# The order of attention on TensorE, planned by a step-by-step model of three engines

## What is computed

```python
qh, kh, vh = heads(layernorm(x) @ Wq.T + bq), heads(ctx @ Wk.T + bk), heads(ctx @ Wv.T + bv)
scores = einsum('bhqd,bhkd->bhqk', qh, kh) * 32 ** -0.5
scores = where(arange(3202)[None, :] <= arange(4096)[:, None], scores, -inf)   # causal
x = x + (einsum('bhqk,bhkd->bhqd', softmax(scores), vh)) @ Wo.T + bo
x = x + ffn(layernorm(x))    # encoder, top-2 of 8 experts, decoder, layernorm
```

## Time and profile before

| | us |
|---|---|
| median of the runs (3) | 3200.46 |
| lowest and highest | 3199.2 and 3202.05 |
| profiled execution, its own time | 3196.54 |
| its span, first to last instruction | 3194.9 |
| TensorE, VectorE, ScalarE, GpSimd busy | 2996.2, 1813.1, 1518.6, 1620.7 |

### The profile page before, as it was taken

The page is one execution under the profiler, slowest core; times in us unless marked ns, Lnnn a source line. Parts: engine busy times, 40 slices in busy tenths (PEclk is TensorE's granted clock), DMA queues, the critical chain, the costliest instruction groups (busy, mean ns, idle before and its releaser), DMA issues. The chain is left out here.

```text
span 3194.9 us, 42271 instructions
## 1 busy us (share of the span) xinstructions
PE 2996.2 (94%) x15688; PEld 1722.8 (54%) x15688; DVE 1813.1 (57%) x3439; ACT 1518.6 (48%) x2861; POOL 1620.7 (51%) x699
## 2 busy tenths in 40 slices
PE   7977999999999999999999999996858999999996
PEld 6865555554455554555544555532644666555653
DVE  3365888875687774788755788701642333233333
ACT  2232355666555666556666556663224333433332
POOL 1011167779567799467787577797531110111110
PEclk9988799999999999999999999997978999999998
DMA  4559234458544559344568344454983110111000
GB/s 184 201 182 269 77 101 115 113 121 177 142 116 105 122 120 208 108 116 101 122 146 170 110 118 98 112 117 122 321 270 89 53 53 1 53 54 53 27 27 14
DMA packets 133283, 384.04 MB, mean 120 GB/s; under 512 B 12224, under 2 KB 28096, under 8 KB 111584
## 3 DMA queue, kind: packets, MB, share of 16 engines
q0 software_dynamic: 36192, 222.05, 26.9%
q1 hardware_dynamic: 90048, 148.07, 17.0%
q10 hardware_dynamic: 6848, 11.31, 1.2%
HBM read 124.03 MB, written 79.17 MB: 64 GB/s over the span
## 5 line engine op out<-in xcount | busy, mean ns | idle before, releaser
L859 ACT ACTIVATE pT<-s_bank 128x512 f32<-128x512 f32 (+5 forms) x2176 | 1088.7, 581 | 722.7 <-PE s_bank L1019 548.0
L878 DVE TENSOR_REDUCE row_max<-m_bank 128x1 f32<-128x512 f32 (+4 forms) x2240 | 1258.5, 626 | 296.0 <-PE m_bank L972 166.0
L797 POOL TENSOR_TENSOR part_sum<-part_sum,pT 128x2048 f32<-128x2048 f32 x236 | 1103.3, 4675 | 119.4 <-ACT pT L859 112.0
L1019 PE MATMUL s_bank<-q_sb,k_sb 104*128 104x512 f32 (+3 forms) x2176 | 864.9, 426 | 18.6 <-ACT pT L859 15.8
L972 PE MATMUL m_bank<-k_sb,q_sb 96*128 96x512 f32 (+4 forms) x2240 | 811.9, 408 | 26.1 <-DMA q_sb<-qT_hi 20.8
L1019 PEld LDWEIGHTS s_bank<-q_sb,k_sb 104*128 104x128 f32 x2176 | 412.8, 192 | 295.9 <-ACT pT L859 205.6
L972 PEld LDWEIGHTS m_bank<-k_sb,q_sb 96*128 96x128 f32 x2240 | 423.7, 196 | 209.5 <-DVE row_max L878 118.9
L1036 PE MATMUL o_bank<-pT,v_sb 128*32 128x512 f32 (+5 forms) x4352 | 503.4, 580 | 0.0
L1421 POOL TENSOR_TENSOR f_var_eps<-f_mean_var,eps 128x4 f32<-128x4 f32 x8 | 1.6, 203 | 583.9 <-DVE f_mean_var L1585 583.9
L797 POOL TENSOR_TENSOR part_sum<-pT 128x2048 f32<-128x2048 f32 x28 | 127.8, 4564 | 266.9 <-ACT pT L859 216.7
L1036 PEld LDWEIGHTS o_bank<-pT,v_sb 128*32 128x32 f32 (+1 forms) x4352 | 114.0, 110 | 231.7 <-issue 146.5
(11 more groups left out here) (196 smaller groups left out, 3371.0 us busy)
## 6 DMA issues: line engine op xcount, KB each, us to landing
moved_sum<-pT POOLq DMA_DIRECT2D x168, 1024.0 KB, 7.0
q_sb<-qT_hi SPq DMA_DIRECT2D x64, 256.0 KB, 5.0
k_sb<-kT_hi SPq DMA_DIRECT2D x48, 256.0 KB, 8.6
qT_hi<-q_hi POOLq DMA_DIRECT2D x8, 1024.0 KB, 6.9
qT_lo<-q_lo POOLq DMA_DIRECT2D x8, 1024.0 KB, 9.0
q_sb<-qT_lo SPq DMA_DIRECT2D x32, 256.0 KB, 4.6
aT<-o_sb ACTq DMA_DIRECT2D x32, 256.0 KB, 5.1
a_in<-aT SPq DMA_DIRECT2D x8, 1024.0 KB, 9.2
```

Source lines behind the costliest of these rows:

```text
L797: pool.tensor_tensor(total, pT[:, slot(S - 1), :, q0:] if j and kt == 1 else total, pT[:, slot(S), :, q0:], ALU.add).then_inc(pool_added, 1)
L859: act.activation(pT[0:rows, slot(S), item, q0:], s_bank[(HG * S + item) % S_RING][0:rows, q0:], ACT.Exp, scale=SCALE).then_inc(exp_done, 1)
L878: dve.tensor_reduce(row_max[:, j % 2, r, h, c:c + 1], m_bank[p % M_BANKS][:, 0:n], AX_X, ALU.max).then_inc(unit_max, 1)
L1019: mm = pe.matmul(out[:, q0:], k_sb[0:R_END, h, at:at + P], q_sb[j % QBUFS][0:R_END, h, q0:], start=True, stop=kt < 4 * j)
```

## The change

The fixed `ORDER` goes. A class `Model` holds the three engines' times, with new constants: what a switch from scores to values and back costs, longer time for negating maxima, shorter time until a result can be read. `schedule` now decides item by item among a score, a bank job (*unit* in the code) and a value group. It computes when each could start, keeps those that could start within 0.03 us of the earliest, and chooses by rules on how much work ScalarE and VectorE still have in hand. A value group may come as soon as its scores are issued, and at the latest when four further scores are. Bank jobs may now run 6.0 us ahead of their wanted time (2.0 before), they press when 1.0 us late (4.0 before), and there is no limit of two in a row. `wanted` and `released` stay as they are. The denominators follow the first value group of the next block, `copy_block` follows the exponential of the first score issued after the block's last value group. The work of each engine, instruction by instruction, stays the same; only its order changes.

```diff
@@ -498,7 +498,7 @@
 
 
 DEN_AFTER, INVERT, SPREAD, NORMALISE, STORE = 2, 1, 2, 3, 7
-SUMS_AT = {ST * g + FIRST_STEP[j + 1] + DEN_AFTER: (g, j) for g in range(NG) for j in range(QB) if (g, j) != (NG - 1, QB - 1)}
+SUMS_BEHIND = {ST * g + FIRST_STEP[j + 1] + DEN_AFTER: (g, j) for g in range(NG) for j in range(QB) if (g, j) != (NG - 1, QB - 1)}
 
 
 def max_units(j):
@@ -523,11 +523,14 @@
 ROWS_BEHIND, ROWS_EARLY = 8, 3
 
 
-ORDER = ((0, 1, 2, "values", 3), (0, 1, 2, 3))
-T_MATMUL, T_MASK, T_VALUES, T_TURN, T_LOAD = 0.235, 0.07, 0.82, 0.1, 0.1
-T_TO_READ, T_TO_WRITE = 0.5, 0.06
+T_MATMUL, T_MASK, T_VALUES, T_TURN = 0.235, 0.06, 0.82, 0.1
+T_TO_VALUES, T_FROM_VALUES, T_SECOND = 0.17, 0.13, 0.1
+T_TO_READ, T_TO_WRITE = 0.28, 0.05
 T_EXP, T_EXP_END, T_MAX, T_MAX_END = 0.48, 0.6, 0.6, 0.68
-T_AHEAD, T_BEHIND = 2.0, 4.0
+T_NEGATE, T_ROWS, T_ROWS_COPY = 2.6, 0.3, 0.52
+T_AHEAD, T_BEHIND = 6.0, 1.0
+VALUES_BEHIND = 4
+T_EXP_LEFT, T_VALUES_LEFT, T_MAX_LEFT = 0.5, 1.4, 0.6
 
 
 def widths(j, kt):
@@ -539,10 +542,11 @@
     t, at = 0, []
     for S, (g, s, j, kt) in enumerate(ALL_STEPS):
         at.append([])
-        for item in ORDER[S % 2]:
-            at[-1].append(t)
+        for item in ((0, 1, 2, 3, "values") if S % 2 else range(HG)):
+            if item != "values":
+                at[-1].append(t)
             if item == "values":
-                t += 2 * T_VALUES * widths(j, kt) + 2 * T_TURN + (4.5 * T_VALUES if S in SUMS_AT else 0)
+                t += 2 * T_VALUES * widths(j, kt) + 2 * T_TURN + (4.5 * T_VALUES if S + 1 in SUMS_BEHIND else 0)
             else:
                 t += T_MATMUL * widths(j, kt) + (T_MASK if kt >= 4 * j else 0)
     return at
@@ -587,66 +591,178 @@
     return at, [job for job, _, _ in jobs], lead, when
 
 
+class Model:
+
+
+    def __init__(self, lead):
+        self.pe = self.act = self.dve = 0
+        self.exp_end, self.bank_end, self.last, self.behind_values = [], [0] * lead, None, 2
+
+    def turn(self):
+
+        if self.last == "values":
+            self.behind_values = 0
+            self.pe += T_FROM_VALUES
+        else:
+            self.behind_values += 1
+            self.pe += T_SECOND if self.behind_values == 1 else 0
+        self.last = "scores"
+
+    def bank_free(self):
+        return max(self.pe, self.bank_end[-M_BANKS] + T_TO_WRITE)
+
+    def score_free(self):
+        return max(self.pe, self.exp_end[-S_RING] + T_TO_WRITE if len(self.exp_end) >= S_RING else 0)
+
+    def values_free(self, v):
+
+        first, second = (self.exp_end[HG * S + HG - 1] + T_TO_WRITE for S in (2 * v, 2 * v + 1))
+        return max(self.pe, first, second - T_VALUES)
+
+    def score(self, j, kt):
+        self.pe = self.score_free()
+        self.turn()
+        self.pe += T_MATMUL * widths(j, kt) + (T_MASK if kt >= 4 * j else 0)
+        self.act = max(self.act, self.pe + T_TO_READ)
+        self.exp_end.append(self.act + T_EXP_END - T_EXP + (T_EXP - 0.06) * widths(j, kt))
+        self.act += 0.06 + (T_EXP - 0.06) * widths(j, kt)
+
+    def unit(self, n, masked, last):
+        self.pe = self.bank_free()
+        self.turn()
+        self.pe += T_MATMUL * n / BLK + (T_MASK if masked else 0)
+        self.dve = max(self.dve, self.pe + T_TO_READ)
+        self.bank_end.append(self.dve + T_MAX_END - T_MAX + 0.07 + (T_MAX - 0.07) * n / BLK)
+        self.dve += 0.07 + (T_MAX - 0.07) * n / BLK + (T_NEGATE if last else 0)
+
+    def rows(self):
+        self.pe = self.bank_free()
+        self.turn()
+        self.pe += T_ROWS
+        self.act = max(self.act, self.pe + T_TO_READ) + T_ROWS_COPY
+        self.bank_end.append(self.act + T_EXP_END - T_EXP)
+
+    def values(self, v):
+        self.pe = self.values_free(v)
+        self.pe += 0 if self.last == "values" else T_TO_VALUES
+        for S in (2 * v, 2 * v + 1):
+            _, _, j, kt = ALL_STEPS[S]
+            self.pe = max(self.pe, self.exp_end[HG * S + HG - 1] + T_TO_WRITE) + T_VALUES * widths(j, kt)
+        self.last = "values"
+
+    def denominators(self, j):
+        own = sum(widths(j, kt) for kt in range(key_tiles(j)) if adder(j, kt) == "matmul")
+        self.pe = self.bank_free() + T_VALUES * (1 + (CHAINS if j else 0) + own) + T_TURN
+        self.dve = max(self.dve, self.pe + T_TO_READ) + T_MAX
+        self.bank_end.append(self.dve + T_MAX_END - T_MAX)
+
+
 def schedule():
 
 
     at, jobs, lead, when = wanted()
-    ring, places, left = jobs[:lead], [], []
+    ring, left = jobs[:lead], []
+    places = [[[] for _ in range(HG)] for _ in ALL_STEPS]
     latest = len(ALL_STEPS)
     for job, t in zip(reversed(jobs[lead:]), reversed(when)):
         if job[0] == "rows":
             latest = ST * job[1] + FIRST_STEP[job[2]] - ROWS_EARLY
         left.insert(0, (job, t, latest))
-    pe = act = dve = 0
-    exp_end, bank_end = [0] * S_RING, [0] * lead
-
-    def do(job):
-
-        nonlocal pe, act, dve
-        kind, g, j, *i = job
...
+    model = Model(lead)
+    n = v = copied_by = copied = 0
+    here = None
+    sums_at, sums = {}, 0
+
+    def slot_free(S):
+
+        if S < SLOTS:
+            return True
+        g, _, j, kt = ALL_STEPS[S - SLOTS]
+        return S - SLOTS < 2 * v and (adder(j, kt) != "matmul" or QB * g + j < sums)
+
+    while n < HG * len(ALL_STEPS) or 2 * v < len(ALL_STEPS) or left:
+        S, h = divmod(min(n, HG * len(ALL_STEPS) - 1), HG)
+        early = left[0][1] - at[S][h] if left else 0
+        must = bool(left) and S >= left[0][2]
+        ready = {}
+        if left and (must or early <= T_AHEAD):
+            ready["unit"] = model.bank_free()
+        if not must and n < HG * len(ALL_STEPS) and slot_free(S):
+            ready["score"] = model.score_free()
+        if 2 * v < len(ALL_STEPS) and n >= max(2 * HG * (v + 1), copied_by):
+            ready["values"] = max(model.values_free(v), copied)
+        overdue = "values" in ready and n >= 2 * HG * (v + 1) + VALUES_BEHIND
+        first = min(ready.values()) + 0.03
+        ready = [kind for kind in ready if ready[kind] <= first]
+        due = "unit" in ready and early <= 0
+        if overdue:
+            kind = "values"
+        elif must or due and early < -T_BEHIND:
+            kind = "unit"
+        elif "score" in ready and model.act - model.pe < T_EXP_LEFT:
+            kind = "score"
+        elif due and model.dve - model.pe < T_MAX_LEFT:
+            kind = "unit"
+        elif "values" in ready and model.act - model.pe >= T_VALUES_LEFT:
+            kind = "values"
+        elif due:
+            kind = "unit"
         else:
-            pe += (4.5 if j else 2.5) * T_VALUES
...
-            while left and (len(ring) - first < 2 or S >= left[0][2]):
-                early = left[0][1] - at[S][k]
-                late = S >= left[0][2] or early < -T_BEHIND
-                if early > T_AHEAD or not late and bank_end[-M_BANKS] + T_TO_WRITE + T_LOAD > pe:
-                    break
-                do(left.pop(0)[0])
-            places[-1].append(range(first, len(ring)))
-    assert not left
+                _, _, _, width, _, masked = UNITS[job[2]][job[3]]
+                model.unit(width, masked, job[3] == len(UNITS[job[2]]) - 1)
+            here.append(("bank", len(ring)))
+            ring.append(job)
+        else:
+            model.pe = max(model.pe, copied)
+            model.values(v)
+            here.append(("values", v))
+            v += 1
+            if 2 * v < len(ALL_STEPS) and ALL_STEPS[2 * v][3] == 0:
+                copied_by = n + 1
+            if 2 * v in SUMS_BEHIND:
+                g, j = SUMS_BEHIND[2 * v]
+                model.denominators(j)
+                here.append(("bank", len(ring)))
+                ring.append(("denominators", g, j))
+                sums += 1
+                sums_at[(n - 1) // HG] = (g, j)
     ring.append(("denominators", NG - 1, QB - 1))
-    return ring, range(lead), places
-
-
-BANK_JOBS, FIRST_JOBS, PLACES = schedule()
+    return ring, range(lead), places, sums_at
+
+
+BANK_JOBS, FIRST_JOBS, PLACES, SUMS_AT = schedule()
+
+
+def bank_places(places):
+    return [p for what, p in places if what == "bank"]
+
+
+def copies_at():
+
+    at = {}
+    for S, places in enumerate(PLACES):
+        for h, here in enumerate(places):
+            for what, v in here:
+                if what == "values" and 2 * v + 2 < len(ALL_STEPS) and ALL_STEPS[2 * v + 2][3] == 0:
+                    g, _, j, _ = ALL_STEPS[2 * v + 1]
+                    at[HG * S + h + 1] = (g, j)
+    return at
+
+
+COPIES_AT = copies_at()
 
 
 def load_keys(sp, kT_hi, kT_lo, k_sb, k_loaded, g, c):
@@ SyncE, VectorE: places are read through bank_places(places)
@@ -853,16 +969,15 @@
                     q0, rows = first_query(j, kt), key_rows(kt)
 
                     reuse_slot(S - SLOTS)
-                    for item, places in zip(ORDER[S % 2], PLACES[S]):
-                        if item in range(HG):
-                            reach(act, s_done, HG * S + item + 1)
```

(54 more changed lines are left out.)

29 lines of the change are left out of this document (1 added, 28 removed).

## The result

The changed kernel is slower: 3238.7 us median (3232.66 to 3243.71) against 3199.83 for the kernel before in the same comparison, ratio 1.012, 95% interval 1.0101 to 1.0139. The forecast was 3178, with a range up to 3210. The profiled execution has a span of 3231.1 us, 36.2 over the one before.

The account below looks back on a forecast made before the run. It took dense pairs as VectorE's as much as TensorE's, and GpSimd as bounding block 7. 49.8 gained less 27.9 lost took 21.9 off 3196.5: 3174.6 profiled, 3178.5 median, range 3138 to 3210.

Parts of the forecast that it names:

- Step 5, keys: Block 7, step (7, 4): a unit placed ahead of its key chunk stalls TensorE; 9.3 us at three borders, 27.9 lost.
- Step 5, the border unit of block 3: Next group's block 0: block 3's first unit may come at step (0, 2); 0, at most 1.5 us each.
- Step 1: Blocks 1 to 5: a better order cuts TensorE and VectorE waiting for each other; 7.2 us a group, 28.8 gained.
- Step 2: Start of a group: 11 more units move from VectorE-bound blocks into block 0; 2.5 us each in three groups, 7.5 gained.
- Step 3: Block 6: can shrink by 4.5 us before TensorE waits for GpSimd; 13.5 gained in three groups, none in the last.
- steps 4 and 6: Stretches without units (4): 0. Copies, sums and the rest (6): 0, with 0 to 16 us if copies held ScalarE.
- The third rival: Scores first behind a value group widen VectorE's gap by 0.335 us in dense pairs; 3231, chance 0.12.
- The second: Rival: dense pairs are VectorE's already, so the better order in blocks 1 to 5 brings next to nothing; 3207, chance 0.21.

Follow-up runs that it names:

- before_wait: The kernel before, order unchanged, with only a TensorE wait for the next group's key chunk added ahead of step (7, 4)'s first score: 3225.55 us, ratio 1.0094.
- warm_wait: The changed kernel with 34 spare matmuls on TensorE ahead of the key chunk wait, in groups 1 to 3: 3229.02 us, ratio 1.01.
- q_border: The changed kernel with units barred until their loads are taken as landed, except those of query block 3: 3197.45 us, ratio 1.0.
- half_max_before: The kernel before with each VectorE maximum taken over the first half of its columns only: 3177.83 us, ratio 0.995.
- guard0_soft: The changed kernel with units barred until their loads are taken as landed, and scores held for overdue units one step later: 3182.12 us, ratio 0.9949.

## Why the prediction was wrong

It named the mechanism that decided, and still forecast the wrong sign. From -21.9 to the +37.6 of the blocks are 59.5 us, which go to the steps so:

1. *Step 5, keys: 27.9 forecast, 35.1 measured.* The place, the length of the wait (9.2 forecast, 8.5 measured), GpSimd as the carrier and the lower clock were right; the size wasn't. The forecast took 1.8 us of slack off each wait. In before_wait that saved nothing: a bare wait of 8.2 us made block 7 longer by 9.7 to 10.4. In the new order a stall costs 11.7. Why it is more than the bare one no run shows. *TensorE: Matmul & The Clock Gate*, "HAM oscillation — how this bites in real kernels", of the Trainium skill, has each burst behind a wait for DMA start at half clock. The trace agrees: value groups of 2.97, 3.64 and 3.64 us for 1.92. The forecast put this clock at 5.7 us; warm_wait gives 6.4, unevenly. Missing 7.2 us.
2. *Step 5, the border unit of block 3: 0 forecast, 12.2 measured in blocks 0.* I wrote that it came at step (0, 2), behind its load by some two value groups, "by either limit". The new list has it one step earlier, behind the last score of (0, 1). The old order ran four scores, a value group and the denominators between that score and the unit, 7.0 us (818.03 to 825.04); its unit started 12.5 us after the request for the queries, and the new one, after its wait, 8.4. The waits are 8.3 of the 12.2 us; of the rest some 3.3 are the half clock behind them, counted over what these blocks had of it before. q_border shows the whole by itself. Missing 12.2.
3. *Step 1: 28.8 forecast, 12.0 measured.* The ceiling of 12.0 us a group came from VectorE's idle time, with TensorE's need taken from one pair of full, unmasked matmuls (6.3 for 6.66 us). VectorE's idle time before the maxima didn't fall at all, 33.0 us for 32.3. half_max_before speaks against VectorE as the bound: with a third of its time gone, the blocks gave 2.4 us, and 5.1 with the new order as well. The same mistake sank my own explanation after the result. What does bound them at some 268 us stays open. I can only argue for masked and narrow units, whose weight loads don't fit beside them, and shape changes; weight loads that wait for ScalarE are as possible. Missing 16.8.
4. *Step 2: 7.5 forecast, none of it seen.* The step needed 11 more units in block 0, and the planner placed none: in groups 1 to 3 its list has 4 units in block 0, before and after. Blocks 1 to 3 of group 1 have 162 for 170, but those eight units went to later blocks. So the leeway that stalled TensorE took no work out of the dense blocks. Missing 7.5.
5. *Step 3: 13.5 forecast, 4.4 measured.* In the three groups that the forecast counted it was 5.8; in the last, block 6 got 1.4 longer. GpSimd's slack of 4.5 us was a bound, not a gain; about 2 us a block came. Missing 9.1.
6. *Not in the forecast: block 2 of group 0, 6.5.* A unit whose bank isn't free has to stand back for scores and value groups until its last step, so the planner falls behind and pays there in one batch at VectorE's pace, with the clock at half behind it. guard0_soft took back 3.4 of it. The remaining 0.2 lie in the start and blocks 0 and 1 of group 0.

Nothing here contradicts steps 4 and 6: the last block, which has no units, came out no longer, and neither was priced by a run of its own. The third rival, at 3231, was nearest to the 3238.7, but for the wrong reason: VectorE's gap behind a value group grew to 0.72 us, not to 0.9. The second was wrong in its mechanism too, since blocks 1 to 5 of group 1 didn't stay at 273 us but came to 269.6.

## What to carry to other kernels

A planner that may run work ahead of its wanted time needs a second limit that never moves: the time at which its data has landed. Under one number for both, a step that was safe becomes a wait in an in-order stream, and everything queued behind pays, down to an engine that has no part in it. Price each wait where its first instruction stands among its neighbours, not by its step, and add what the clock takes behind it. And before an idle engine's time is called recoverable, shorten that engine's work in a run: if the stretch doesn't shrink, the bound is elsewhere.

## What the hardware showed that I had not expected

At the border of block 3 waits of 2.3, 3.6 and 2.4 us, each in an otherwise thin stretch, all came with a fall to the 1.2 GHz clock, which lasted into the work behind. In group 1 the value group and the first denominators behind took 3.21 and 1.61 us for 1.92 and 1.04. A wait isn't needed for it: in the kernel before, block 0 of group 2 had a granted clock of 0.71, though no wait of TensorE there was over 0.7 us. Keeping TensorE busy with spare matmuls through an 8 us wait held the clock at 2.4 GHz, in all three groups. The key chunk's three DMAs, 256 KB each, took 8.4 us from the first request to the unit's start, near the 9.2 of the kernel before.
